# Where the next values are made: moving small steps of a fused attention and expert kernel around its last batch

## The chip, the cores and the metric

One core of one Trainium2 chip. The metric is the device time of one launch in microseconds, median of three runs.

## The reference

One model step on 16 sequences of 256 tokens, width 128, in float32: a long convolution, a mixture of experts, an attention, and the same mixture of experts again, each added to its input after a layer norm.

```python
x = x + conv(layernorm(x), ...)          # state-space convolution by FFT
x = x + ffn(layernorm(x), ...)           # 8 experts, hidden 256, top 2 of a softmax
x = x + attention(layernorm(x), ...)     # 16 heads of 8, 4 query sets, causal
x = x + ffn(layernorm(x), ...)           # the same experts

# ffn
w, idx = top_k(softmax(x @ Wg + bg), 2);  w = w / sum(w)
comb = sum(one_hot(idx) * w)
h = relu(einsum(x, W1) + b1);  y = einsum(h, W2) + b2
out = einsum(y, comb)
# attention: for each of 4 query sets, with shared keys and values
att = softmax(causal(q @ k.T * scale));  y = att @ v
out = concat(y) @ W_proj.T
```

## The kernel before

The 4096 tokens are 32 tiles of 128. All intermediate data stays in the core's memory. Each engine runs one long list of instructions, written out by hand in the order of its queue; semaphores with constant thresholds connect them. There is no planner. The phases are: filter taps and convolution, the first expert pass, the attention, and the second expert pass.

**Expert passes** (`tensor_first`, `tensor_second` and their like on the other engines). 8 chunks of 4 tiles, 8 experts each. For an expert PE runs `tensor_up` (L718, two halves of three matmuls, into PSUM banks 0 to 3), ScalarE `scalar_relu` (L732 and L734, four instructions), VectorE and GpSimd form low parts (L741, L748), and two experts later PE runs `tensor_down` (L766, 24 matmuls of 128 columns, into banks 4 and 5 in turn), which VectorE adds into `mixed`, weighted by `comb_y` (`vector_accumulate`, L778). `tensor_down` waits for the accumulation two experts before, and each accumulation for the one before it. Between the experts of a chunk stand the routing steps of the next: norm statistics (`vector_route_stats`, L324 and L328), a reciprocal root on GpSimd (`gpsimd_route_rstd`, L333 and L335), `vector_route_normed` (L341), transposition (`tensor_xt`, L591), `tensor_logits` (L616), `vector_top` (L623 to L634), an exponential of the gap (`scalar_gap`, L639), `vector_combine` (L645 to L667), `tensor_comb_t` (L676), its copy `scalar_comb_t` (L684), the biases weighted by the router (`tensor_base`, L691) and their addition to the stream (`vector_base`, L699). Chunk 0 of the second pass has no pass of its kind before it, so its routing steps stand in the last batch element of the attention.

**Attention** (`tensor_attention` and its like). 16 batch elements, 16 steps each, numbered n from 0 to 255. A step on PE: `tensor_scores(n)` (L1013, three matmuls of 512 columns) into banks 0 to 2 or 3 to 5 in turn, which waits until ScalarE is done with step n - 2; then what stands beside it (`tensor_beside`); then the weighing of the values of four steps earlier (`tensor_weigh`, L1064, into bank 7): none at n % 4 == 0, one, two and one at the following steps. ScalarE runs one `scalar_exp` (L1022, 128x1536) for each step, GpSimd masks its result (L1032 to L1040), VectorE turns the outputs of four steps (`vector_turn`, L1072 to L1077) at n % 4 == 3, and the next weighing waits for the turn. Scores 1 wait for the last accumulation of the first pass, since its output stands in bank 5.

**Beside the steps** of batch element b, by step number: the transposition of element b + 2 at 0 (`tensor_at_x`, L865, which waits until the values of b are copied out of bank 6), its queries and keys at 4, 8 and 12 (`tensor_qk`, L906, and on VectorE `vector_qk_high` L931 and `vector_qk_low` L936), the output projection of element b - 1 at 7 and 11 (`tensor_project`, L1119, `vector_attended`, L1129), and the values of element b + 1 at 14:

```python
        if b + 1 < BATCH and at == 14:
            tensor_v(e, b + 1)
```

`tensor_v` (L970, six matmuls into bank 6) waits for the last `vector_qk_low`, and `vector_v` (L989) copies its result. In the last element the projections stand at 10 and 11. Norm statistics and normalization of later chunks stand beside these steps too.

**Seam to the second pass.** `tensor_second` weighs the last four sums with `tensor_up(0, 0)` and `tensor_up(0, 1)` between them, and projects the last element after expert 2 of chunk 0.

Of the kernel before, what the change touches and what calls it, by code (L numbers as in the profile page):

```python
# [17 lines left out]
P = 128  # L18
# [98 lines left out]
def build_in(nc, dr, out, ctx):  # L117
# [523 lines left out]
    def vector_combine(e, m, ch):  # L641
# [13 lines left out]
        last.then_inc(routed, 1)  # L655
        e.wait_ge(routed, at + 9)
# [10 lines left out]
        e.tensor_scalar(comb_y[:, s], comb[:, s], 1.0 if m.whole else 1.0 / WSCALE, None, ALU.mult).then_inc(routed, 1)  # L667

# [81 lines left out]

    def tensor_down(e, m, ch, ex):
        i = (m.at + ch) * EXPERTS + ex
        r, to = i % HRING, bank(4 + i % 2)
# [8 lines left out]
        if i >= 2:  # L762
            e.wait_ge(accum, i - 1)
        for t in range(FFN_TILES):
# [5 lines left out]
    def vector_accumulate(e, m, ch, ex):  # L770
# [6 lines left out]
        for t in range(FFN_TILES):  # L777
            last = e.scalar_tensor_tensor(out=m.y[:, t0 + t, :], in0=bank(4 + i % 2)[:, t * P:(t + 1) * P],  # L778
# [217 lines left out]
    def tensor_scores(e, n):  # L996
        b, c, t = step_of(n)
        s, to = b % 2, psum[:, TILE * (n % 2):TILE * (n % 2 + 1)]
        if n >= 2:
            e.wait_ge(exped, n - 1)  # L1000
        elif n == 1:
            e.wait_ge(accum, EXPERTS * FFN_CHUNKS)
        else:
            e.wait_ge(relued, HBLK * EXPERTS * FFN_CHUNKS)
# [45 lines left out]
    def tensor_weigh(e, n):  # L1050
# [5 lines left out]
        if n == 0:  # L1056
            e.wait_ge(based, FFN_CHUNKS)
# [48 lines left out]
    def tensor_project(e, b, h):  # L1106
# [5 lines left out]
        elif b + 3 == BATCH:  # L1112
            e.wait_ge(attn_done, HALVES * b + 1)
        elif b + 2 == BATCH:
            e.wait_ge(combt_copied, FFN_CHUNKS + 1)
# [7 lines left out]
    def vector_attended(e, b, h):  # L1123
        tile = HALVES * b + h

        e.wait_ge(projected, tile + 1 if b + 2 < BATCH else HALVES * (b + 1))
# [239 lines left out]
    def tensor_second(e):  # L1366
# [8 lines left out]
        for ch in range(FFN_CHUNKS):  # L1375
            for ex in range(EXPERTS):
                if ch or ex >= 2:
                    tensor_up(e, second, ch, ex)
                if due := lagging(ch, ex):
# [16 lines left out]
    def scalar_second(e):  # L1396

        e.wait_ge(scored, LAST)
        for ch in range(FFN_CHUNKS):
            for ex in range(EXPERTS):  # L1400
                scalar_relu(e, second, ch, ex)
                if ch + 1 < FFN_CHUNKS:
                    scalar_route(e, second, ch + 1, routing_step(ch + 1, ex))

    def vector_second(e):
        for ch in range(FFN_CHUNKS):
            for ex in range(EXPERTS):
                vector_low(e, second, ch, ex)
                if (ch, ex) == (0, 0):
                    vector_turn(e, LAST // 4 - 1)  # L1410
                    vector_rows(e, BATCH - 1)
                if due := lagging(ch, ex):
# [10 lines left out]
                if (ch, ex) == (1, 4):  # L1423
                    vector_route_stats(e, second, FFN_CHUNKS - 1)
                if (ch, ex) == (1, 7):
                    vector_route_normed(e, second, FFN_CHUNKS - 1)
# [13 lines left out]
    def gpsimd_second(e):  # L1440
        for ch in range(FFN_CHUNKS):
            for ex in range(EXPERTS):
                gpsimd_low(e, second, ch, ex)
                if (ch, ex) == (1, 5):
                    gpsimd_route_rstd(e, second, FFN_CHUNKS - 1)
# [15 lines left out]
    def tensor_beside(e, b, at):  # L1461
# [6 lines left out]
        if b + 1 < BATCH and at == 14:  # L1468
            tensor_v(e, b + 1)
        if b + 1 == BATCH:  # L1470
# [5 lines left out]
            elif at == 8:  # L1476
                tensor_comb_t(e, second, 0)
            elif at in (10, 11):
                tensor_project(e, b - 1, at - 10)
            elif at == 14:  # L1480
# [372 lines left out]
```

## Time and profile before

| | |
|---|---|
| median of 3 runs | 875.84 us (875.54 to 876.68) |
| profiled execution | 874.92 us |
| its span, first to last instruction | 873.2 us |
| granted TensorE clock, mean over the span | 0.992 of 2.4 GHz |
| busy: PE / ScalarE / VectorE / GpSimd | 94% / 83% / 75% / 63% |
| first pass, attention, second pass start at about | 95, 291, 670 us |

PE is TensorE's matmuls, PEld its weight loads, DVE VectorE, ACT ScalarE, POOL GpSimd, SP SyncE. Times in the trace are microseconds from the start of the span. Matmuls are pipelined and their ends modelled, so a listed duration can run into the next instruction. An idle time in brackets is that of the engine before the instruction, with the instruction that ended it. Rows of busy time by stretch list the stretch, its length, the busy microseconds and number of instructions of PE, PEld, DVE, ACT and POOL, the granted TensorE clock as a share of 2.4 GHz, the DMA engines' share and GB/s.

### The profile page before, as it was taken

What the parts mean: (1) busy time and instruction counts of PE and PEld (TensorE: products, weight loads), DVE (VectorE), ACT (ScalarE), POOL (GpSimd) and SP (SyncE); (2) the same over time, 40 slices, a digit from 0 to 9 for tenths busy, and PEclk for the clock granted to TensorE, in tenths of its full rate; (3) what the DMA queues carried; (4) which work ended last, traced back from release to release, by engine and by line L of the source; (5) the groups of instructions that cost most, each with busy time, mean ns of one, the idle gap of its engine ahead of it and who ended that gap; (6) DMA issues with size and microseconds to landing.
All of it is one profiled execution on the core that took longest, in us unless ns stands there. A gap on an engine that the chain in (4) does not pass through costs nothing.

```text
span 873.2 us, 20943 instructions
## 1 busy us (share of the span) xinstructions
PE 825.0 (94%) x7953; PEld 465.6 (53%) x7953; DVE 657.1 (75%) x1966; ACT 727.7 (83%) x918; POOL 549.7 (63%) x620
## 2 busy tenths in 40 slices
PE   5899999999999899999999999999989999999995
PEld 4644577777777433333333333333223777777774
DVE  6898689988987566777777777777565888777775
ACT  7630588888898799999999999999997788988884
POOL 1177455555543688888888888888885454444432
PEclk9999999999999899999999999999999999999999
DMA  8101100000003334434444433355300000000000
GB/s 282 33 1 48 49 2 2 2 2 2 2 16 84 98 82 92 85 93 83 98 90 98 90 83 85 96 99 98 97 1 2 2 14 14 14 14 13 14 14 15
DMA packets 38408, 46.00 MB, mean 53 GB/s; under 512 B 6680, under 2 KB 24352, under 8 KB 38304
## 3 DMA queue, kind: packets, MB, share of 16 engines
q1 hardware_dynamic: 38304, 44.62, 21.5%
q8 instruction: 64, 1.05, 0.6%
q14 instruction: 40, 0.33, 0.1%
HBM read 27.83 MB, written 16.78 MB: 51 GB/s over the span
## 4 chain that ended last, share of the span: by engine, by line
PE 69%; DVE 13%; ACT 10%; issue 4%; POOL 2%; SPq 0%; DMA 0%; ACTq 0%
PE psum L766 18%; PE psum L718 17%; PE psum L1064 13%; ACT prob L1022 7%; PE psum L1013 5%; PE psum L1119 4%; DVE normed L341 3%; PE psum L545 2%; POOL prob L1037 2%; ACT decay L409 2%; PE psum L906 2%; DVE o_tok L1072 2%; PE psum L691 2%; PE psum L616 1%; PE psum L512 1%
## 5 line engine op out<-in xcount | busy, mean ns | idle before, releaser
L1022 ACT ACTIVATE prob<-psum 128x1536 f32<-128x1536 f32 x256 | 349.7, 1474 | 26.7 <-PE psum L1013 26.7
L1064 PE MATMUL psum<-prob,vstack 128*32 128x256 f32 (+1 forms) x2048 | 206.9, 499 | 2.6 <-DVE o_tok L1072 2.6
L718 PE MATMUL psum<-xt_parts,w_parts 128*128 128x512 f16 x768 | 186.8, 379 | 0.0
L778 DVE SCALAR_TENSOR_TENSOR mixed<-psum,comb_y,mixed 128x128 f32<-128x128 f32 x512 | 143.5, 342 | 2.1 <-PE psum L766 2.1
L748 POOL TENSOR_TENSOR hidden_parts_second<-hidden_second,hidden_parts_second 128x512 f16<-128x512 f32 x64 | 78.0, 1219 | 104.5 <-ACT hidden_parts_second L734 104.5
L748 POOL TENSOR_TENSOR hidden_parts_first<-hidden_first,hidden_parts_first 128x512 f16<-128x512 f32 x64 | 80.0, 1253 | 82.6 <-ACT hidden_parts_first L734 82.6
L732 ACT ACTIVATE hidden_first<-psum,b 128x512 f32<-128x512 f32 x128 | 88.2, 689 | 26.7 <-PE psum L718 19.1
L1032 POOL TENSOR_SCALAR_AFFINE_SELECT prob<-prob 128x512 f32<-128x512 f32 x128 | 82.4, 644 | 43.7 <-ACT prob L1022 38.3
L732 ACT ACTIVATE hidden_second<-psum,b 128x512 f32<-128x512 f32 x128 | 88.4, 691 | 25.2 <-PE psum L718 23.8
L1013 PEld LDWEIGHTS psum<-qstack,kstack 32*128 32x128 f16 x768 | 24.8, 91 | 157.0 <-ACT prob L1022 117.2
L1013 PE MATMUL psum<-qstack,kstack 32*128 32x512 f16 x768 | 100.9, 390 | 8.0 <-POOL prob L1037 3.6
L718 PEld LDWEIGHTS psum<-xt_parts,w_parts 128*128 128x128 f16 x768 | 71.3, 99 | 65.4 <-issue 2.2
L1072 DVE STREAM_TRANSPOSE o_tok<-psum 128x512 f32<-128x512 f32 x64 | 45.8, 716 | 71.5 <-PE psum L1064 71.4
L766 PEld LDWEIGHTS psum<-w_parts,hidden_parts_first 128*128 128x128 f16 x1536 | 90.9, 98 | 16.1 <-issue 1.9
L766 PEld LDWEIGHTS psum<-w_parts,hidden_parts_second 128*128 128x128 f16 x1536 | 91.0, 98 | 15.2 <-issue 0.6
L766 PE MATMUL psum<-w_parts,hidden_parts_first 128*128 128x128 f16 x1536 | 96.0, 219 | 0.7 <-DVE mixed L778 0.6
L766 PE MATMUL psum<-w_parts,hidden_parts_second 128*128 128x128 f16 x1536 | 96.0, 219 | 0.5 <-POOL hidden_parts_second L748 0.5
L1037 POOL TENSOR_SCALAR_AFFINE_SELECT prob<-prob 128x1280 f32<-128x1280 f32 x64 | 85.1, 1330 | 5.8 <-ACT prob L1022 1.2
L734 ACT ACTIVATE hidden_parts_second<-psum,b 128x512 f16<-128x512 f32 x128 | 88.5, 692 | 0.0
L734 ACT ACTIVATE hidden_parts_first<-psum,b 128x512 f16<-128x512 f32 x128 | 88.3, 690 | 0.0
L1034 POOL TENSOR_SCALAR_AFFINE_SELECT prob<-prob 128x512 f32<-128x512 f32 x128 | 82.5, 645 | 0.0
L741 DVE TENSOR_TENSOR hidden_parts_second<-hidden_second,hidden_parts_second 128x512 f16<-128x512 f32 x64 | 44.9, 702 | 42.2 <-ACT hidden_parts_second L734 42.1
(116 smaller groups left out, 1110.2 us busy)
## 6 DMA issues: line engine op xcount, KB each, us to landing
qstack<-qk_parts SPq DMA_DIRECT2D x128, 128.0 KB, 3.6
qk_parts<-parts SPq DMA_DIRECT2D x64, 192.0 KB, 3.2
kstack<-qk_parts SPq DMA_DIRECT2D x128, 32.0 KB, 3.6
stream<-L_attn_a_u SPq DMA_DIRECT2D x4, 512.0 KB, 7.5
kept_x<-stream SPq DMA_DIRECT2D x4, 512.0 KB, 2.6
out<-mixed SPq DMA_DIRECT2D x8, 256.0 KB, 2.3
w_whole<-L_ffn_W SPq DMA_DIRECT2D x1, 1024.0 KB, 7.4
taps<-c_taps SPq DMA_DIRECT2D x1, 640.0 KB, 8.4
```

The costliest lines, as they stand in the source:

```text
L718: last = e.matmul(bank(u % 4), m.w1[:, w_part, ex, cols], xt_parts[:, s, x_part, :], start=(n == 0), stop=(n == len(PRODUCTS) - 1))
L732: last = e.activation(m.hidden[:, r, k, :], bank(u % 4), ACT.Relu, scale=scale, bias=bias)
L734: last = e.activation(m.hidden_parts[:, r, 0, k, :], bank(u % 4), ACT.Relu, scale=scale, bias=bias)
L748: e.tensor_tensor(m.hidden_parts[:, r, 1, 1, :], m.hidden[:, r, 1, :], m.hidden_parts[:, r, 0, 1, :], ALU.subtract).then_inc(low_second, 1)
L766: last = e.matmul(to[:, t * P:(t + 1) * P], h_[:, t * P:(t + 1) * P], w_, start=(n == 0), stop=(n == len(terms) - 1))
L778: last = e.scalar_tensor_tensor(out=m.y[:, t0 + t, :], in0=bank(4 + i % 2)[:, t * P:(t + 1) * P], scalar=comb_y[:, s, t, ex:ex + 1], in1=m ...
L1013: last = e.matmul(to[:, i * BANK:(i + 1) * BANK], kstack[at, s, c, keys * P:(keys + 1) * P], queries, start=True, stop=True)
L1022: e.activation(prob[:, n % PROBS, :], psum[:, TILE * (n % 2):TILE * (n % 2 + 1)], ACT.Exp, scale=SCALE)\
L1032: e.affine_select(blocks[:, 0:3:2], blocks[:, 0:3:2], [[0, 2], [0, 2], [1, P]], ALU.is_ge, 0.0, base=0, channel_multiplier=-1)
L1034: e.affine_select(blocks[:, 4:6], blocks[:, 4:6], [[0, 2], [0, 2], [1, P]], ALU.is_ge, 0.0, base=0, channel_multiplier=-1).then_inc(masked, 1)
L1037: e.affine_select(blocks[:, 0:5], blocks[:, 0:5], [[0, 5], [0, 2], [1, P]], ALU.is_ge, 0.0, base=0, channel_multiplier=-1).then_inc(masked, 1)
L1064: last = e.matmul(to[SLOT * lane:SLOT * (lane + 1)], vstack[:, b % 2, keys, first:first + SLOT], weights_of(n - t, lane, keys, pair), star ...
```

## The change

Five edits to the order of the queues and one to a buffer:

- `tensor_v` of the next element stands beside step 15 instead of 14. VectorE's copy stays in its list at step 14, in front of the turn of step 15.
- The output of the last `tensor_down` of the first pass goes to bank 7 instead of 5 (`down_bank`). Scores 1 wait for one accumulation less, the first weighing for all.
- In the last element the projections stand at 8 and 11, and each attended tile waits for its own projection. `vector_combine` is cut in two, `vector_pick` at step 8 and `vector_comb` at step 12.
- `tensor_comb_t`, `scalar_comb_t`, `tensor_base` and `vector_base` of the second pass's chunk 0 move into the second pass, at its experts 0 and 1.
- The norm of chunk 6 moves from the last element into chunk 0 of the second pass (statistics at expert 4, root at 5, normalization at 7), as that of chunk 7 already stood in chunk 1.

```diff
+    def down_bank(m, i):
+        return 7 if m is first and i == EXPERTS * FFN_CHUNKS - 1 else 4 + i % 2
...
     def tensor_down(e, m, ch, ex):
         i = (m.at + ch) * EXPERTS + ex
-        r, to = i % HRING, bank(4 + i % 2)
+        r, to = i % HRING, bank(down_bank(m, i))
...
+        if down_bank(m, i) == 7:
+            e.wait_ge(based, FFN_CHUNKS)
...
     def tensor_scores(e, n):
         elif n == 1:
-            e.wait_ge(accum, EXPERTS * FFN_CHUNKS)
+            e.wait_ge(accum, EXPERTS * FFN_CHUNKS - 1)
...
     def tensor_weigh(e, n):
         if n == 0:
-            e.wait_ge(based, FFN_CHUNKS)
+            e.wait_ge(accum, EXPERTS * FFN_CHUNKS)
...
     def tensor_project(e, b, h):
+        elif b + 2 == BATCH and h == 0:
+            e.wait_ge(routed, STEPS * FFN_CHUNKS + 1)
         elif b + 2 == BATCH:
-            e.wait_ge(combt_copied, FFN_CHUNKS + 1)
+            e.wait_ge(attn_done, HALVES * b + 1)
...
     def vector_attended(e, b, h):
-        e.wait_ge(projected, tile + 1 if b + 2 < BATCH else HALVES * (b + 1))
+        e.wait_ge(projected, tile + 1 if b + 1 < BATCH else HALVES * (b + 1))
...
     def tensor_second(e):
+                if (ch, ex) == (0, 0):
+                    e.wait_ge(attn_done, HALVES * (BATCH - 1))
+                    tensor_comb_t(e, second, 0)
+                if (ch, ex) == (0, 1):
+                    tensor_base(e, second, 0)
...
     def scalar_second(e):
                 scalar_relu(e, second, ch, ex)
+                if (ch, ex) == (0, 0):
+                    scalar_comb_t(e, second, 0)
...
     def vector_second(e):
+                if (ch, ex) == (0, 1):
+                    vector_base(e, second, 0)
...
-                if (ch, ex) == (1, 4):
-                    vector_route_stats(e, second, FFN_CHUNKS - 1)
-                if (ch, ex) == (1, 7):
-                    vector_route_normed(e, second, FFN_CHUNKS - 1)
+                if ch < 2 and ex == 4:
+                    vector_route_stats(e, second, FFN_CHUNKS - 2 + ch)
+                if ch < 2 and ex == 7:
+                    vector_route_normed(e, second, FFN_CHUNKS - 2 + ch)
...
     def gpsimd_second(e):
-                if (ch, ex) == (1, 5):
-                    gpsimd_route_rstd(e, second, FFN_CHUNKS - 1)
+                if ch < 2 and ex == 5:
+                    gpsimd_route_rstd(e, second, FFN_CHUNKS - 2 + ch)
...
     def tensor_beside(e, b, at):
-        if b + 1 < BATCH and at == 14:
+        if b + 1 < BATCH and at == 15:
             tensor_v(e, b + 1)
...
-            elif at == 8:
-                tensor_comb_t(e, second, 0)
-            elif at in (10, 11):
-                tensor_project(e, b - 1, at - 10)
-            elif at == 14:
-                e.wait_ge(attn_done, HALVES * (BATCH - 1))
-                tensor_base(e, second, 0)
+            elif at in (8, 11):
+                tensor_project(e, b - 1, at // 10)
...
     def scalar_attention(e):
-            elif n == LAST - STEPS_B + 8:
-                scalar_comb_t(e, second, 0)
...
     def vector_beside(e, b, at):
-        if 0 < b < BATCH - 1 and at in (6, 10):
-            vector_attended(e, b - 1, at // 8)
-        if b + 1 == BATCH and at in (9, 10):
-            vector_attended(e, b - 1, at - 9)
+        if b and at in (6 if b + 1 < BATCH else 9, 10):
+            vector_attended(e, b - 1, at // 10)
...
-        if b % 2 and b >= 3:
+        if b % 2 and 3 <= b < BATCH - 1:
...
-            elif at == 6:
-                vector_combine(e, second, 0)
-            elif at == 14:
-                vector_base(e, second, 0)
+            elif at == 8:
+                vector_pick(e, second, 0)
+            elif at == 12:
+                vector_comb(e, second, 0)
```

## Rows read from the trace of the kernel before

**Rows 1.** Busy time by stretch: batch 1, last batch, a second-pass chunk.

```profile
338.23:361.37 23.14, 22.33 (x219) 8.17 (x215) 16.91 (x38) 21.81 (x16) 20.03 (x27) 1.00 0.45 92
640.53:670.07 29.54, 24.88 (x228) 8.97 (x227) 19.87 (x57) 23.95 (x21) 22.24 (x29) 0.94 0.01 2
694.30:718.30 24.00, 24.00 (x254) 17.84 (x252) 20.76 (x78) 19.81 (x36) 13.15 (x11) 1.00 0.05 13
```

**Rows 2.** Timeline of ScalarE: start, duration, operation, idle time before.

```profile
315.10 12.20 ACT L1022 ACTIVATE prob<-psum 128x1536 f32<-128x1536 f32 x9 [0.50 <-PE psum L1013]
...
356.85 4.13 ACT L1022 ACTIVATE prob<-psum 128x1536 f32<-128x1536 f32 x3 [0.66 <-PE psum L1013]
361.37 12.20 ACT L1022 ACTIVATE prob<-psum 128x1536 f32<-128x1536 f32 x9 [0.39 <-PE psum L1013]
...
593.86 12.20 ACT L1022 ACTIVATE prob<-psum 128x1536 f32<-128x1536 f32 x9 [1.04 <-PE psum L1013]
```

**Rows 3.** Timeline around step 14 of batch 1, PE and VectorE.

```profile
358.68 0.69 DVE L936 SCALAR_TENSOR_TENSOR parts<-psum,parts 128x512 f16<-128x512 f32 x1
...
359.43 0.51 PE L970 MATMUL psum<-wqkv_parts,at_x 128*128 128x128 f16 x6 [0.61 <-DVE parts L936]
...
359.87 1.07 PE L1064 MATMUL psum<-prob,vstack 128*32 128x256 f32 x16
...
360.87 0.39 PE L1013 MATMUL psum<-qstack,kstack 32*128 32x512 f16 x3
...
361.19 1.07 PE L1064 MATMUL psum<-prob,vstack 128*32 128x512 f32 x8
```

**Rows 4.** Timeline at the seam from the first pass to the attention.

```profile
294.05 0.61 PE L1013 MATMUL psum<-qstack,kstack 32*128 32x512 f16 x6 [1.00 <-DVE mixed L778]
...
299.81 1.94 PE L1064 MATMUL psum<-prob,vstack 128*32 128x512 f32 x8
...
302.34 12.26 ACT L1022 ACTIVATE prob<-psum 128x1536 f32<-128x1536 f32 x9 [0.96 <-PE psum L1013]
```

**Rows 5.** Busy time by stretch: attention's start, small operations of the last batch.

```profile
295.00:300.00 5.00, 3.27 (x19) 1.23 (x23) 1.56 (x8) 5.00 (x5) 3.79 (x6) 0.55 0.44 101
649.94:652.04 2.10, 2.10 (x29) 0.70 (x27) 2.00 (x7) 1.74 (x2) 2.10 (x4) 0.87 0.00 0
```

**Rows 6.** Timeline of the last batch, from step 6 on.

```profile
649.94 0.84 DVE L645 CAST top_no<-top_at 128x8 f32<-128x8 uint32 x1
...
650.24 4.30 ACT L1022 ACTIVATE prob<-psum 128x1536 f32<-128x1536 f32 x3 [0.41 <-PE psum L1013]
...
654.52 0.60 PE L676 MATMUL psum<-eye,comb 128*8 128x128 f32 x4 [1.56 <-DVE comb L665]
...
657.27 1.16 PE L1119 MATMUL psum<-wproj,o_rows 128*128 128x128 f32 x8
...
659.86 1.45 ACT L1022 ACTIVATE prob<-psum 128x1536 f32<-128x1536 f32 x1 [0.96 <-PE psum L1013]
...
668.64 1.50 PE L1064 MATMUL psum<-prob,vstack 128*32 128x512 f32 x16 [0.84 <-DVE o_tok L1072]
```

**Rows 7.** Timeline: comb_t's copy, the last projections, the biases of chunk 1.

```profile
655.16 0.57 ACT L684 COPY comb_t<-psum 8x512 f32<-8x512 f32 x1 [0.62 <-PE psum L676]
...
677.47 2.05 PE L1119 MATMUL psum<-wproj,o_rows 128*128 128x128 f32 x16 [0.23 <-DVE o_rows L1087]
...
694.37 1.15 PE L691 MATMUL psum<-b,comb_t 8*128 8x128 f32 x8
```

**Rows 8.** Timeline of the second pass: accumulation and statistics.

```profile
690.99 1.11 DVE L778 SCALAR_TENSOR_TENSOR mixed<-psum,comb_y,mixed 128x128 f32<-128x128 f32 x4
...
692.93 1.50 PE L766 MATMUL psum<-w_parts,hidden_parts_second 128*128 128x128 f16 x24
...
712.20 0.86 DVE L324 BATCH_NORM_STATS2 stats<-stream 128x6 f32<-128x128 f32 x4
713.10 0.38 DVE L328 BATCH_NORM_AGGREGATE meanvar<-stats 128x2 f32<-128x6 f32 x4
```

More of the change, by code:

```diff
@@ L639, in scalar_gap, with vector_pick @@
         e.activation(gap[:, s, :], gap[:, s, :], ACT.Exp).then_inc(gap_exp, 1)
-    def vector_combine(e, m, ch):
+    def vector_pick(e, m, ch):
         n, s = m.at + ch, ch % 2
@@ L655, in vector_combine, with vector_comb @@
         last.then_inc(routed, 1)
+    def vector_comb(e, m, ch):
+        n, s = m.at + ch, ch % 2
+        at = STEPS * n
         e.wait_ge(routed, at + 9)
@@ L667, in vector_combine @@
         e.tensor_scalar(comb_y[:, s], comb[:, s], 1.0 if m.whole else 1.0 / WSCALE, None, ALU.mult).then_inc(routed, 1)
+    def vector_combine(e, m, ch):
+        vector_pick(e, m, ch)
+        vector_comb(e, m, ch)
     def tensor_comb_t(e, m, ch):
@@ L777, in vector_accumulate @@
         for t in range(FFN_TILES):
-            last = e.scalar_tensor_tensor(out=m.y[:, t0 + t, :], in0=bank(4 + i % 2)[:, t * P:(t + 1) * P],
+            last = e.scalar_tensor_tensor(out=m.y[:, t0 + t, :], in0=bank(down_bank(m, i))[:, t * P:(t + 1) * P],
                                           scalar=comb_y[:, s, t, ex:ex + 1], in1=m.y[:, t0 + t, :], op0=ALU.mult,
@@ L1557, in gpsimd_attention @@
                 gpsimd_mixed_rstd(e, b // 2 + 2)
-            if at == 3 and b % 2 and b >= 3:
+            if at == 3 and b % 2 and 3 <= b < BATCH - 1:
                 gpsimd_route_rstd(e, second, (b - 3) // 2)
```

## The prediction

> **What bounds the kernel now.** I read the page first, then the busy time by stretch, then ScalarE's timeline through the attention, and only then all engines around the places that the diff touches.
>
> The attention is 256 steps, 16 to a batch element (a "batch" below). A step is one `scalar_exp` of 1.45 us on ScalarE. A batch lasts 23.14 us, of which ScalarE is busy 21.81 and PE 22.33 [rows 1]: both are nearly full, so the question is which is late at each step. ScalarE's rows answer it: the exps come in unbroken runs, and each run begins with an idle time that ended with L1013, the scores on PE [rows 2]. Three exps in a row last 4.13, so one follows the next after (4.13 - 1.45) / 2 = 1.34 us; they overlap by 0.11, and a pause costs its listed idle time plus 0.11. So ScalarE sets the end, and PE adds a pause wherever it had too much work between two scores. A PE step is 0.32 for the scores (360.87 to 361.19) and 1.00 for the weighing (359.87 to 360.87) [rows 3]; every fourth step has no weighing. An exp starts 0.50 after its scores (360.87 to 361.37). A listed PE duration runs some 0.07 into the next instruction (1.07 against 1.00), which I take off below.
>
> One pause of each batch stands where the change works. At step 14 PE stands 0.61 us until L936 has made the low parts, then runs the six matmuls of the next values (L970, 0.44 to the next instruction), then the weighing, and only then the scores of step 15 [rows 3]. Exp 15 starts at 361.37, with 0.39 idle before it [rows 2].
>
> The last batch is another case: 29.54 us up to the second pass's first matmul, at a mean clock of 0.94. A chunk of the second pass has PE busy through all of its 24.00 us, with VectorE at 20.76 [rows 1]. What is added to PE there counts in full; what is added elsewhere counts where PE comes to wait.
>
> **Part 1, values in step 15.** I count from the start of exp 12 (356.85). Without its stand, PE would begin the product at 359.43 - 0.61 - 0.07 = 358.75. With the product gone from there, the weighing begins then and scores 15 come 1.00 later, at 2.9. Exp 15 could start at 3.4; its turn on ScalarE is 3 x 1.34 = 4.03, and in the rows it starts at 4.52. So the pause goes if step 15 can carry the product: 2.9 + 0.32 + 0.44 + 1.00 puts scores 16 at 4.7, exp 16 could start at 5.2 and is due at 5.37. It fits, with 0.18 to spare. The low parts are ready at 2.5 (358.68 + 0.69) [rows 3], before the product's new place at 3.2, so the stand goes too. In step 16 the next transposition needs the copied values: the copy (a VectorE instruction of some 0.4, an estimate from 128x512 in 0.69) ends at about 4.2, the transposition comes at 5.0. VectorE now stands for the copy in front of the turn. The turn waits for the weighing of step 15, which ends at 4.7, so the copy is done by then, and nothing else is queued between.
>
> The saving is one pause in each of the batches 0 to 13; 14 and 15 have no product that waits for L936. The first costs 0.50 + 0.11. In batch 12 VectorE is late with L936 through the weight ranges, and the pause costs 1.04 + 0.11; L936 is ready there some 0.65 later than elsewhere, at 3.2, just in time for the new place. The twelve others cost 0.39 + 0.11 [rows 2]. 0.61 + 1.15 + 12 x 0.50 = **-7.8 us**. Bounds: nothing, if the pause only moves; 7.8, if none is left.
>
> **Part 2, last outputs in bank 7.** Scores 1 stand 1.00 us for the last accumulation of pass one, because its bank is one of theirs [rows 4]. With that output in bank 7 they wait for the one before, which is done: 1.00 earlier. The weighing that now waits for bank 7 comes at 299.81, long after. But the gain meets a slow clock: TensorE's granted clock is 0.55 on average from 295 to 300 [rows 5], so 1.2 GHz for most of it. The weighing takes 1.94 instead of 1.07, and exp 6 starts at 302.34 after 0.96 idle [rows 4]. If the slow stretch stays in its place, one more microsecond of PE work falls into it, and by exp 7 some 0.4 of the 1.0 is left. I take **-0.6** (0.4 to 1.0).
>
> **Part 3, the last batch.** Removed from it: comb_t at step 8 with PE's wait of 1.56 for VectorE, its copy on ScalarE, the biases, VectorE's share of them, and the norms of chunk 6. The two projections (1.16, so 1.09) move from steps 10 and 11 to 8 and 11. I walk it from exp 6 at 650.24 [rows 6]. Three exps take 4.30 there, so exp 8 starts at 653.09 and its scores at 652.6. Step 8 is now 0.32 + 1.09: scores 9 at 654.0, exp 9 at 654.5, 0.07 late. Steps 9 and 10 are 1.32 each: exp 10 at 655.8, exp 11 at 657.2. Step 11 is 0.32 + 1.09 + 1.00: scores 12 at 659.05, exp 12 at 659.55, a pause of 1.04, such as a projection makes today (0.96 idle at 659.86). PE goes on: step 12 (no weighing) to 659.4, the wait for the turn to 660.1, steps 13 to 15 to 663.8, and the wait for the turn in front of the last matmuls as now (0.84 idle in its row, 0.9 with the overlap): 664.7 in place of 668.64, **-3.9 us**. It needs VectorE to be done with the picks and the first attended tile when the projection comes at 657.0. The turn of step 7 should end there at about 654.2; VectorE's work from 649.94 to 652.04, mostly these small operations, is 2.1 us [rows 5], so they end at 656.3 and the tile at 656.6. Bounds: -2.9, if they take a microsecond more; -4.9, if the clock stays full in this batch.
>
> The page "SBUF — State Buffer" of the Trainium skill (section "Who interferes with whom") has a rule against this step: a VectorE instruction with two SBUF inputs, or a cast in a two-port mode, and a GpSimd one that reads SBUF shut each other out, each for the whole of the other. The cast at 649.94 takes 0.84 for 8 elements a partition, with GpSimd busy throughout, which agrees. By the rule alone each of three picks could stand behind a whole mask, and the projection would be a microsecond late: the sum would be 1 us higher. By the row it is not.
>
> **Part 4, comb_t and biases in the second pass.** They now stand on PE between the attention's last weighing and `tensor_up(0, 2)`. From comb_t's start to the start of its copy are 0.64 (654.52 to 655.16), the copy takes 0.57, and PE goes on some 0.2 later: 1.4. Nothing of PE's queue can pass this wait. The biases take 1.15, 1.08 net [rows 7]. Of these 2.5 us, what PE stands today before the last projections is hidden: 0.23 in the row of 677.47, about 0.4 with the overlap. **+2.1 us** (1.7 to 2.6). ScalarE stands too, because the copy is queued between relu 0 and relu 1; but relu 1 is next wanted by `tensor_up(0, 3)`, two ups, a down and two projections later. VectorE's addition of the biases is in time for chunk 1's transposition, for the same reason.
>
> **Part 5, norms in the second pass.** Statistics and aggregation cost VectorE 0.86 + 0.38 = 1.24 at expert 4, behind `vector_combine` in the same expert. Today the accumulation of expert 3 ends at 690.99 + 1.11 = 692.1, and `tensor_down` of expert 5, which waits for it, starts at 692.93 [rows 8]: 0.83 to spare. 1.24 - 0.83 = 0.4, with contention **+0.5** (0 to 1.2). The normalization at expert 7 precedes nothing that PE wants soon, and GpSimd, with 13.15 busy of 24.00 [rows 1], has room for its two operations.
>
> **The sum** is -7.8 - 0.6 - 3.9 + 2.1 + 0.5 = -9.7 us. The profiled execution took 874.92 (span 873.2 and 1.7 around it), 0.9 under the median of 875.84 and 0.6 under the fastest of the three. -9.7 gives 865.2 for a profiled run and **866.1 us** for the median.
>
> **Rivals.** (a) *The pause moves instead of closing.* If the product takes 0.7 in step 15 instead of 0.44, or the transposition of step 16 stands for the copy, exp 16 is late by what exp 15 gained, in each batch, and the 7.8 is lost: 873.9. For it: the margin of 0.18. Against: scores, product and weighing have their measured lengths, and the copy has 0.8 to spare.
>
> (b) *More is lost at the seam.* The picks are late, or TensorE's clock falls to 1.2 GHz in the thin work of part 4 (a stand, small matmuls). At the other seam it was at 1.2 GHz soon after PE stood 1.00 [rows 4, 5], and a weighing took 0.87 longer; in a part that PE bounds this costs 1 to 1.7. With one or both, +2.3: 868.4.
>
> The skill's page "TensorE: Matmul & The Clock Gate" (section "Why this matters for your kernels") ties a fall to a long idle gap between bursts of matmuls. The stand at 294.05 was short, so the trace doesn't agree that only long ones matter. By the page the clock part of this rival costs nothing; by the row it can.
>
> (c) *Slower: the clock falls in every batch.* PE's stand and its work change places in step 14 and 15. If that takes the clock to 1.2 GHz once a batch, each fall costs a pause as in rows 4, 0.96 + 0.11 = 1.07; fourteen are +15.0, and the sum is +5.3: 881.1. It decides from ten falls on. Against: the clock is 1.00 in a whole batch [rows 1] in spite of a stand of 0.61, which now goes away.
>
> **Chances.** The forecast 0.74 (own range 863.8 to 869, by the bounds above without all of them at once), (b) 0.15, (a) 0.08, in part or in full, (c) 0.03. The range 863.5 to 870.3 leaves out (c), most of (a) and some of the low end. Within 0.2% (1.8 us) this kernel can't be told from no change; (a) in full stands at that limit. Faster 0.93, same 0.04, slower 0.03.
>
> **What would show it.** A batch takes 22.6 us in place of 23.14, with two pauses (exps 8 and 12) instead of three, and L970 has no idle time before it. Scores 1 start at 293.0. From the first exp of the last batch to `tensor_up(0, 0)` it is 25.6 instead of 29.5. Then PE stands some 0.9 us before L691, and the second pass takes 2.6 more than today. The forecast is wrong if a pause appears before exp 16, if the last batch has pauses beside the one at its exp 12, or if the clock is under 1 in the second pass.

## The result and the profile after

The changed kernel takes **863.0 us** (median of 6 runs, 861.68 to 864.4), the kernel before 876.37 beside it (6 runs, 875.54 to 876.96): a ratio of 0.9848, interval 0.9836 to 0.9861, or 13.4 us less. Forecast were 866.1 and a range from 863.5; the direction was right, the gain 3.7 too small and outside the range.

The profiled execution took 863.78 us (span 862.0, mean granted clock 0.992), 11.1 less than that of before. So two profiles differ by 2.3 us less than the medians do, and that gap is most of what has to be explained. Three executions among all the runs below, two of the kernel before (1048.9 and 1361.55 us) and one of the changed kernel with added matmuls (2047.37 us), were slow and are left out of the ratios.

Busy time by stretch: batch 1 (counted, as in [rows 1], from its exp 15 to the next batch's exp 15), the attention's start, and the last batch from its first exp to `tensor_up(0, 0)`. They answer to [rows 1, 5]. Counted from exp 0, the step in [rows 3] is one of batch 2 and not of batch 1; the batches are alike there.

```profile
335.04:357.68 22.64, 22.34 (x219) 8.18 (x215) 17.10 (x39) 21.70 (x18) 19.95 (x27) 1.00 0.48 94
295.00:300.00 5.00, 4.05 (x23) 1.24 (x23) 1.99 (x8) 4.99 (x4) 4.80 (x7) 0.66 0.40 116
630.81:656.24 25.43, 23.33 (x217) 7.75 (x215) 13.55 (x44) 23.06 (x20) 21.07 (x27) 0.93 0.00 1
```

ScalarE's timeline, from exp 1 and in the last batch [rows 2, 4, 6]:

```profile
293.10 6.89 ACT L1036 ACTIVATE prob<-psum 128x1536 f32<-128x1536 f32 x5 [0.74 <-PE psum L1027]
300.27 24.32 ACT L1036 ACTIVATE prob<-psum 128x1536 f32<-128x1536 f32 x18 [0.28 <-PE psum L1027]
324.87 5.48 ACT L1036 ACTIVATE prob<-psum 128x1536 f32<-128x1536 f32 x4 [0.28 <-PE psum L1027]
331.01 16.23 ACT L1036 ACTIVATE prob<-psum 128x1536 f32<-128x1536 f32 x12 [0.66 <-PE psum L1027]
347.52 5.48 ACT L1036 ACTIVATE prob<-psum 128x1536 f32<-128x1536 f32 x4 [0.28 <-PE psum L1027]
...
640.48 8.33 ACT L1036 ACTIVATE prob<-psum 128x1536 f32<-128x1536 f32 x6 [0.41 <-PE psum L1027]
649.73 5.48 ACT L1036 ACTIVATE prob<-psum 128x1536 f32<-128x1536 f32 x4 [0.92 <-PE psum L1027]
```

Where [rows 2] have runs of 3 and 9 exps with 0.39 between, there is now one of 12 (331.01): the pause before exp 15 is gone, and none came before exp 16. Exp 6 starts after 0.28 idle instead of 0.96. In the last batch the 0.41 before exp 6 is as it was, and the only other pause is one of 0.92 before its exp 12.

PE's timeline, the last batch's weighing and projections, then the seam and the accumulation behind the norm's statistics [rows 6 to 8]:

```profile
637.90 1.94 PE L1078 MATMUL psum<-prob,vstack 128*32 128x512 f32 x8
...
643.09 1.16 PE L1136 MATMUL psum<-wproj,o_rows 128*128 128x128 f32 x8
...
647.14 1.16 PE L1136 MATMUL psum<-wproj,o_rows 128*128 128x128 f32 x8
...
654.80 1.50 PE L1078 MATMUL psum<-prob,vstack 128*32 128x512 f32 x16 [0.84 <-DVE o_tok L1086]
...
660.60 0.60 PE L684 MATMUL psum<-eye,comb 128*8 128x128 f32 x4
...
661.87 1.15 PE L699 MATMUL psum<-b,comb_t 8*128 8x128 f32 x8 [0.66 <-ACT comb_t L692]
...
681.49 1.50 PE L780 MATMUL psum<-w_parts,hidden_parts_second 128*128 128x128 f16 x24 [0.32 <-DVE mixed L792]
```

PE stands nowhere for the router in the attention any more, and one weighing took 1.94 instead of 1.07: in this execution the clock was at 1.2 GHz there. VectorE's small operations of the router at step 8, behind the turn, with `comb` of step 12, and what GpSimd did beside the first of them:

```profile
642.90 0.72 DVE L1086 STREAM_TRANSPOSE o_tok<-psum 128x512 f32<-128x512 f32 x1 [2.03 <-PE psum L1078]
...
644.53 0.16 DVE L645 CAST top_no<-top_at 128x8 f32<-128x8 uint32 x1
...
645.38 0.72 DVE L653 TENSOR_TENSOR pick<-expert_no,top_no 128x32 f32<-128x32 f32 x2
646.02 0.28 DVE L1146 TENSOR_TENSOR stream<-psum,mixed 128x128 f32<-128x128 f32 x1
...
651.17 0.19 DVE L669 TENSOR_TENSOR comb<-pick 128x32 f32<-128x32 f32 x1
```

```profile
643.46 0.87 POOL L1054 TENSOR_SCALAR_AFFINE_SELECT prob<-prob 128x768 f32<-128x768 f32 x1
644.80 0.64 POOL L1046 TENSOR_SCALAR_AFFINE_SELECT prob<-prob 128x512 f32<-128x512 f32 x1 [0.47 <-ACT prob L1036]
```

Cut at the same events (exps 0, 6, 15 and 240, the second pass's first up, first down and sixth down), the difference of the two profiles is: part 1 (exps 15 of batches 0 to 13) -7.7, part 2 (exp 0 to exp 6) -1.7, last batch -4.1, comb_t and biases in the second pass +1.9, norm +0.5, sum -11.1. The last two can't be parted in this pair: from the first up to the first down it is 2.35 longer, from there to the sixth down 0.05. They are parted by the run further down that moves comb_t and the biases and not the norm: +2.35 and -0.44 there, so +0.49 is left for the norm.

### The profile page after: what moved, and what is told of

Its sections match the earlier page's. It is cut to its first block, busy times and chain, and to the rows that moved or that the text cites. A ratio compares the mean times of both kernels' runs of the same rounds, so it can differ in the third digit from the quotient of the medians.

```text
span 862.0 us, 20945 instructions
## 1 busy us (share of the span) xinstructions
PE 824.6 (96%) x7953; PEld 465.9 (54%) x7953; DVE 655.3 (76%) x1966; ACT 726.0 (84%) x918; POOL 550.8 (64%) x620
## 4 chain that ended last, share of the span: by engine, by line
PE 66%; ACT 14%; DVE 9%; issue 7%; POOL 3%; SPq 0%; DMA 0%; ACTq 0%
PE psum L780 17%; PE psum L726 16%; PE psum L1078 12%; ACT prob L1036 11%; PE psum L1027 5%; PE psum L1136 4%; DVE normed L341 3%; PE psum L545 2%; POOL prob L1051 2%; PE psum L920 2%; PE psum L699 2%; PE psum L616 1%; DVE mixed L792 1%; PE psum L512 1%; DVE prod L524 1%
```

## The experiments

**Each part alone.** Three kernels, each with one group of the edits, and one with all but part 2.

```diff
e1_values (part 1)
-        if b + 1 < BATCH and at == 14:
+        if b + 1 < BATCH and at == 15:
             tensor_v(e, b + 1)
e2_bank7 (part 2)
-        r, to = i % HRING, bank(4 + i % 2)
+        r, to = i % HRING, bank(down_bank(m, i))
...
-            e.wait_ge(accum, EXPERTS * FFN_CHUNKS)
+            e.wait_ge(accum, EXPERTS * FFN_CHUNKS - 1)
e3_seam (parts 3 to 5): projections at 8 and 11, pick at 8, comb at 12,
        comb_t, biases and the norm of chunk 6 in the second pass
e4_no_bank7: the changed kernel without the edits of e2_bank7
```

> The kernel before with tensor_v in step 15 alone (part 1). Sum of the pauses: 7.8 us less, so a ratio of 0.991, in the median as in the profile, with L970 without idle time and no pause before exps 15 and 16. If the 3.7 us that the changed kernel gained beyond the forecast come from part 1, more than 9 us less. If they come from the seams and TensorE's clock there, exactly 7.8, and the same slow stretches as before (near 295 and near 647 less the shift).

> The kernel before with the last outputs of pass one in bank 7 alone (part 2). By the forecast 0.6 us less (0.4 to 1.0). By the theory that PE's stand of 1.00 at the seam is what lets the clock fall for so long, 1.7 or more: scores 1 come 1.00 earlier, the slow stretch is half as long, and exp 6 has 0.3 idle before it instead of 0.96. A median that gains more than the profile would say that the slow stretch is missing in some executions.

> The kernel before with the edits of the last batch and the second pass (parts 3, 4 and 5) and nothing else. By the forecast -3.9 + 2.1 + 0.5 = 1.3 us less; by the profile of the changed kernel -4.1 + 1.9 + 0.5 = 1.7 less. If the surplus of the median lies in the clock of this seam, 2.5 to 4 less in the median.

> The changed kernel without bank 7: parts 1, 3, 4 and 5. If the parts add up, e1 and e3 together: 9.1 us less than before by the forecast, 9.5 by the profile. Against the changed kernel it shows bank 7 once more: 0.6 slower by the forecast, 1.7 to 3.5 slower by the clock theory.

| | median us (runs) | ratio to before, interval |
|---|---|---|
| part 1 alone | 867.72 (6) | 0.99, 0.9887 to 0.9914 |
| part 2 alone | 874.86 (11) | 0.9984, 0.9975 to 0.9993 |
| parts 3 to 5 alone | 872.47 (5) | 0.9959, 0.9945 to 0.9973 |
| all but part 2 | 864.97 (4) | 0.9874, 0.9859 to 0.9889 |

Against 876.53 beside them these are -8.8, -1.7, -4.1 and -11.6. The parts add up to -14.6 against the -13.4 of all, and part 1 and parts 3 to 5 to -12.9 against the -11.6 of the kernel with both; most of what is too much lies in part 1, for which the interval (-9.9 to -7.5) holds the forecast as well. Part 2 is worth -1.7 alone (interval -2.2 to -0.6) and -2.0 (863.0 - 864.97) on top of the rest, where -0.6 was forecast. Parts 3 to 5 are -4.1 together, where the sum had -3.9 + 2.1 + 0.5 = -1.3: here lies the largest miss. The profile of part 1 alone had a last batch of 32.44, though nothing in it was edited; that of parts 3 to 5 one of 24.13.

**Matmuls to hold the clock.** If the miss is the clock, matmuls put where PE stands should hold it. They are added to both kernels: four of 512 columns beside each of steps 2 and 3, and in the last batch at step 2, in the kernel before also at step 0. Their results are not used.

```diff
+            if n == 0:
+                e.wait_ge(based, FFN_CHUNKS)
+                tensor_fill(e, 7)
+            if n in (2, 3):
+                e.wait_ge(accum, EXPERTS * FFN_CHUNKS)
+                tensor_fill(e, 7)
+            if n == LAST - STEPS_B + 2:
+                e.wait_ge(xt_high, FFN_CHUNKS + 1)
+                tensor_fill(e, 6)
```

> The kernel before with extra matmuls, whose results nobody reads, where PE stands at the two seams: four of 512 columns into bank 7 at steps 0, 2 and 3 of the attention, and four into bank 6 at step 2 of the last batch. They cost 0.86 us each time at full clock, where ScalarE sets the pace. By the clock theory the slow stretches at the seams get rarer and the kernel gets faster by 1 to 3 us with a mean clock above 0.994. If TensorE's clock has no share in it, no change, or up to 2 us slower.

> The changed kernel with the same extra matmuls, except at step 0, where bank 7 is in use. By the clock theory it gains less than the kernel before does by them, 0 to 1.5 us, because it has fewer slow stretches, and the distance between the two filled kernels is 10 to 11.5 us, what the queues alone give, in place of 13.4. If the distance stays at 13.4, the surplus is none of the clock.

Before with them: 875.49 (12 runs; ratio 0.9995, 0.9986 to 1.0005), which can't be told from no change, where 1 to 3 us less were expected. Changed with them: 862.35 (6 runs; 0.9844, 0.9828 to 0.986). The distance stayed at 13.1; it did not shrink to the expected 10 to 11.5. By the words of the expectation that speaks against the clock, but the profiles show that the matmuls missed the place where it falls. In both the clock is 1.00 from the first exp on through 15 steps (21.89 us for them in the kernel before, against 23.86 and 23.17 in two profiles without), but the old last batch still took 31.09 at a mean clock of 0.95. These matmuls held the clock at the first seam and, in the new order, in the last batch (24.13, clock 1.00), not in the old order, where it falls later, behind step 8. So something in that order, behind step 8, goes with the fall there; what it is, the next runs show.

**Comb_t behind the first up; the values' product twice.** Two checks on single terms, in the changed kernel.

```diff
e7_combt_early, tensor_second:
         tensor_up(e, second, 0, 0)
+        e.wait_ge(attn_done, HALVES * (BATCH - 1))
+        tensor_comb_t(e, second, 0)
         tensor_weigh(e, LAST - 2)
...
e9_twice, tensor_v:
-        for h in range(HALVES):
+        for h in (0, 1, 0, 1):
```

> The changed kernel with tensor_comb_t behind tensor_up(0, 0), so that ScalarE copies it right after relu 0 and the biases find it ready. The stand of PE before the biases (0.66) and of ScalarE before the copy (1.68) should go: 1.2 us less (part 4 then costs 1.1 instead of 2.35). If part 4's price is PE's own work alone, no gain.

> The changed kernel with the value product made twice over, 12 matmuls instead of 6 (0.44 us more in step 15). By the walk of step 15 it has 0.18 us to spare: exp 16 comes 0.26 late in each of 14 batches, 3.6 us, and the product of the first pass costs 0.4 once: 4 us slower in all. If the step had no room, 14 x 0.44 = 6.2 slower; if PE had room beyond the walk, less than 1.

Comb_t early: 862.81 (0.9846, 0.9828 to 0.9865). From the first up to the first down are 7.19 in place of 8.02: 0.8 is there in the profile, where 1.2 were expected; the medians differ by 0.2, less than they can tell. Product twice: 865.1 (0.9876, 0.9858 to 0.9894), +2.1 and not +4. From exp 16 to exp 240, 14 batches, the profile is 1.62 longer, 0.12 each, for 0.44 more work. Step 15 has 0.44 - 0.12 = 0.32 to spare, not 0.18.

**Comb_t moved alone.** Every profile of the old order shows PE standing at step 8 for VectorE's router result. In the kernel before, only comb_t, its copy and the biases go to the second pass; two more runs are the kernel before and the changed kernel again.

```diff
     tensor_beside, last batch
-            elif at == 8:
-                tensor_comb_t(e, second, 0)
...
     tensor_second
+                if (ch, ex) == (0, 0):
+                    e.wait_ge(attn_done, HALVES * (BATCH - 1))
+                    tensor_comb_t(e, second, 0)
...
```

> The kernel before with one thing alone: comb_t, its copy and the biases of the second pass's chunk 0 stand in the second pass; the router's combination stays whole at step 6, the projections at 10 and 11, the norm of chunk 6 in the attention. Theory (the last batch fell to 1.2 GHz in one or two stretches because PE stood some 2 us for comb_t there): with that stand gone the last batch takes 25 to 25.5 us from its first exp to the second pass's first up, with no slow stretch behind its step 9, part 4 gives 2 back, and the median is 3.5 to 4 under the kernel before. Rival (only the order of the work counts, as in the forecast's sum): 1.5 to 2 under it, with a slow stretch still in the last batch.

> The kernel before once more, for another look at its last batch. Theory (the profiled execution was a lucky one): 31 to 32.5 us from the batch's first exp to the second pass's first up. Rival (29.5 is what this kernel does, and the three other looks at the old order owe their 31 to 32.4 to their own edits): 29.5 again.

> The changed kernel once more, for another look at its last batch: 24.1 with no stretch at 1.2 GHz or 25.4 with one, never above 26, if the old order alone had the longer ones.

The theory fell: **878.98** (12 runs; 1.0023, 1.0011 to 1.0035), slower than before by 2.6, where 3.5 to 4 less was expected. Its profile is 2.3 longer than that of the kernel before again (878.7 against 876.4). The last batch is 0.9 of a microsecond shorter (30.18 against 31.07), the second pass pays the 1.9 of part 4, and 1.2 more lie behind the last down of the kernel, where nothing was edited. PE's timeline in that run:

```profile
652.36 0.39 PE L1013 MATMUL psum<-qstack,kstack 32*128 32x512 f16 x3 [0.37 <-ACT prob L1022]
655.75 1.53 PE L1064 MATMUL psum<-prob,vstack 128*32 128x512 f32 x8 [2.99 <-DVE o_tok L1072]
657.21 0.61 PE L1013 MATMUL psum<-qstack,kstack 32*128 32x512 f16 x3
657.75 2.04 PE L1119 MATMUL psum<-wproj,o_rows 128*128 128x128 f32 x8
```

and VectorE's:

```profile
648.41 1.24 DVE L1087 STREAM_TRANSPOSE o_rows<-o_norm 128x1024 f32<-128x1024 f32 x1
...
649.74 0.84 DVE L645 CAST top_no<-top_at 128x8 f32<-128x8 uint32 x1
...
651.84 1.15 DVE L658 TENSOR_TENSOR pick<-pick,wpair 128x32 f32<-128x32 f32 x2
653.02 1.25 DVE L665 TENSOR_TENSOR comb<-pick 128x32 f32<-128x32 f32 x1
654.30 0.78 DVE L667 TENSOR_SCALAR comb_y<-comb 128x32 f32<-128x32 f32 x1
654.99 0.70 DVE L1072 STREAM_TRANSPOSE o_tok<-psum 128x512 f32<-128x512 f32 x1
```

PE no longer waits for comb, so it waits 2.99 us for the turn instead, which is queued on VectorE behind the whole of `vector_combine`: ten instructions, from 649.74 to 655.08. Several of them last until a mask of GpSimd beside them ends. These are the masks beside `comb` and `comb_y`:

```profile
652.90 1.32 POOL L1037 TENSOR_SCALAR_AFFINE_SELECT prob<-prob 128x1280 f32<-128x1280 f32 x1
654.18 0.86 POOL L1040 TENSOR_SCALAR_AFFINE_SELECT prob<-prob 128x768 f32<-128x768 f32 x1
```

The addition that starts at 653.02 ends 0.05 behind the first mask, at 654.27; in the changed kernel, where no mask runs at its start (651.17), it takes 0.19. The stand was not comb_t's alone; it is VectorE's queue at steps 6 and 7. Behind the stand the projection takes 2.04 instead of 1.16. The kernel before, profiled again, shows the same with comb_t in front:

```profile
654.28 0.60 PE L676 MATMUL psum<-eye,comb 128*8 128x128 f32 x4 [2.32 <-DVE comb L665]
...
655.71 1.57 PE L1064 MATMUL psum<-prob,vstack 128*32 128x512 f32 x8 [0.51 <-DVE o_tok L1072]
...
657.76 2.00 PE L1119 MATMUL psum<-wproj,o_rows 128*128 128x128 f32 x8
```

Its last batch took 31.07 (31 to 32.5 was expected, 29.5 by the rival), that of the changed kernel again 25.42.

**Which edit removes the stand.** From both sides: the cut of the combination added to the last kernel, taken out of the changed one, and taken out while the order behind the turn is kept.

```diff
e11_cut (on e10_combt_moved), and e12_whole the reverse (on the changed kernel)
-            elif at == 6:
-                vector_combine(e, second, 0)
+            elif at == 8:
+                vector_pick(e, second, 0)
+            elif at == 12:
+                vector_comb(e, second, 0)
e13_whole_at_8 (on the changed kernel)
             elif at == 8:
-                vector_pick(e, second, 0)
-            elif at == 12:
-                vector_comb(e, second, 0)
+                vector_combine(e, second, 0)
```

> The kernel before with comb_t and the biases in the second pass (as in the run just before) and, beyond that, one edit: the router's combination is cut in two, its picks at step 8 and the rest at step 12 of the last batch, behind the turns. Projections stay at 10 and 11, the norm of chunk 6 in the attention. Theory (VectorE's uncut combination at step 6 held the turn of step 7, and PE stood for whichever of the two it wanted first): PE's stand of 2.99 at step 8 goes, the last batch takes 25 to 27 us in place of 30.2, with no slow stretch of the clock behind step 9, and the median is 4 under the run with comb_t moved, 873 to 875.5. Rival (the projections' places or the norm made the last batch long): it stays at 29 or more, and the median at 877 or more.

> The changed kernel with one edit undone: the combination whole at step 6, in front of the turn of step 7. Theory: the turn ends some 3 us late, PE stands for it at step 8, and the clock falls behind the stand; the last batch takes 28 to 30 us in place of 24.1 to 25.4, the median is 3.5 to 5.5 above the changed kernel, 866.5 to 868.5. Rival (the projections' new places did it): within 0.7 of the changed kernel, 863 to 863.7.

> The changed kernel with the combination whole, but at step 8, behind the turn of step 7: only the cut is undone, not the order. If the order behind the turn is what counts, the last batch takes 24 to 26 us and the median is 0 to 1.3 above the changed kernel, 863 to 864.3. If the cut counts (three more operations of up to 1.25 beside the masks, in front of the attended tile for which the second projection waits), PE stands at step 11 and it is 2 or more above, 865 or more.

| | median us (runs) | ratio to before, interval | last batch us | PE's longest stand for VectorE in it |
|---|---|---|---|---|
| comb_t moved | 878.98 (12) | 1.0023, 1.0011 to 1.0035 | 30.18 | 2.99, turn |
| + cut | 874.9 (11) | 0.998, 0.9971 to 0.9988 | 26.83 | 1.42, turn |
| changed, whole at 6 | 868.32 (6) | 0.9898, 0.9881 to 0.9916 | 28.50 | 2.83, turn |
| changed, whole at 8 | 867.45 (4) | 0.9888, 0.9873 to 0.9902 | 28.24 | 2.65, attended tile |
| changed | 863.0 (6) | 0.9848, 0.9836 to 0.9861 | 25.43 | 0.84, turn |

The cut alone gives back 4.1 by the medians, its undoing costs 5.3, and keeping only the order costs 4.4 (by the ratios 3.8, 4.4 and 3.5). Each is as the theory or, for the last, the second of its two branches had it, and in each pair the two intervals don't meet. The last batch alone shows it too: 3.35 shorter with the cut, 3.9 and 3.7 longer without it than the mean of 24.6 in the changed order (below). The last batches of the first four, by stretch, in the order of the table:

```profile
640.36:670.54 30.18, 23.61 (x216) 8.46 (x214) 19.43 (x56) 23.01 (x20) 22.39 (x29) 0.94 0.00 1
```

```profile
640.10:666.93 26.83, 22.04 (x217) 7.66 (x214) 19.75 (x56) 22.98 (x20) 22.38 (x29) 1.00 0.01 1
```

```profile
633.03:661.53 28.50, 23.54 (x216) 7.82 (x214) 15.47 (x44) 23.01 (x20) 20.97 (x27) 0.94 0.00 1
```

```profile
632.86:661.10 28.24, 23.54 (x217) 7.92 (x214) 16.07 (x44) 22.80 (x20) 21.13 (x27) 0.94 0.00 1
```

PE in the kernel with the combination whole at 6, then at 8:

```profile
648.32 1.25 PE L1078 MATMUL psum<-prob,vstack 128*32 128x512 f32 x8 [2.83 <-DVE o_tok L1086]
...
650.04 1.94 PE L1078 MATMUL psum<-prob,vstack 128*32 128x256 f32 x16
```

```profile
650.62 1.45 PE L1136 MATMUL psum<-wproj,o_rows 128*128 128x128 f32 x8 [2.65 <-DVE stream L1146]
652.00 1.94 PE L1078 MATMUL psum<-prob,vstack 128*32 128x512 f32 x8
```

Whole at 6, it stands in front of the turn; whole at 8, in front of the first attended tile, for which the second projection waits. Only in two pieces, at steps 8 and 12 with both attended tiles between them, does PE wait for neither. At 8 the ten instructions lie beside masks again, such as this cast, which ends 0.02 behind the mask beside it:

```profile
645.26 1.05 POOL L1054 TENSOR_SCALAR_AFFINE_SELECT prob<-prob 128x768 f32<-128x768 f32 x1
...
645.50 0.83 DVE L645 CAST top_no<-top_at 128x8 f32<-128x8 uint32 x1
```

The way from the old order to the new runs in three steps through the last batch: 31.07, with comb_t moved 30.18, with the cut 26.83, and with the projections at 8 and 11 and the norm gone as well (the run of parts 3 to 5) 24.13. The cut is the largest step, not the whole; the last one, 2.7, was not parted further.

In each case a stand of over 2 us is followed by matmuls at 1.2 GHz and a mean clock of 0.94; without one it is 1.00 (+ cut).

**A better version?** From the changed kernel, comb_t behind the first up and the norm's statistics one expert later; and in a second kernel comb_t in the stand of 0.84 before the last weighings.

```diff
e8_both (on e7_combt_early)
-                if ch < 2 and ex == 4:
+                if (ch, ex) in ((0, 5), (1, 4)):
                     vector_route_stats(e, second, FFN_CHUNKS - 2 + ch)
...
e14_stand (on e8_both), tensor_second
+        e.wait_ge(attn_done, HALVES * (BATCH - 1))
+        tensor_comb_t(e, second, 0)
         tensor_weigh(e, LAST - 4)
...
```

> The changed kernel with comb_t behind the first up of the second pass and the statistics of chunk 6's norm one expert later, its root too. By the single terms: 0.8 for comb_t (its profile showed that) and 0.4 for the statistics, so 1.2 under the changed kernel, 861.8; 0 to 0.4 if the accumulations behind the statistics are late at expert 5 as they were at expert 4.

> The best version so far (comb_t behind the first up, the norm's statistics one expert later) with comb_t moved on into the place in front of the last two weighings of step 255, where PE stands 0.84 us for the turn, and its copy in front of the first relu. Its matmuls (0.53) are then hidden and the copy's wait too: 0.5 under that version, 861.7. Rival: nothing is gained if the copy makes the first relu late or the turn's wait grows.

862.27 (5 runs; 0.9838, 0.9825 to 0.9851) and 862.35 (5 runs; 0.9832, 0.9817 to 0.9846), where 861.8 and 861.7 were expected. In the profiles the terms are there: first up to first down 8.02, 7.19 and 6.76, and 0.49 for the statistics. The medians are 0.7 below the changed kernel's and can't be told from it: between the executions of one kernel, taken over all kernels, the time rises by some 0.4 us for each 0.001 that the mean granted clock is lower, and the same kernel's executions lie between 0.991 and 0.997.

## Why the prediction was wrong, by its steps

| step | forecast | measured |
|---|---|---|
| part 1, values in step 15 | -7.8 | -7.7 by the profiles, -8.8 by the medians |
| part 2, bank 7 | -0.6 | -1.2 by the mean of the profiles, -1.7 and -2.0 by the medians |
| part 3, last batch | -3.9 | -6.5 by the mean of the profiles |
| part 4, comb_t and biases | +2.1 | +1.9 |
| part 5, norm | +0.5 | +0.5 |
| sum | -9.7 | -13.0 by the profiles; medians -13.4 |

**The step that failed is part 3's term.** Its walk forward was right: 25.6 to `tensor_up(0, 0)`, measured 25.43 in the first profile of the changed kernel; projections at steps 8 and 11 on time; a pause of 1.04 at exp 12, measured 0.92 idle and 0.11; 0.84 before the last weighings. That it agrees so closely is in part luck, since this profile has the slow stretch around step 5 that the walk took over from [rows 6], and six of nine don't. What was wrong is the length from which it was taken, -3.9 where the profiles have -6.5. The 29.5 of [rows 1] belong to one execution. Five profiles of the old last batch gave 29.51, 31.07 (before again), 32.44 (part 1 alone), 31.37 (part 2 alone) and 31.09 (with fillers): mean 31.1.

Nine at the new order gave 25.43, 25.42 and 25.49 (comb_t early), and six from 24.09 to 24.13 (one of them with fillers): mean 24.6. The difference is -6.5; of the 2.6 beyond the forecast 1.6 are the old order's (31.1 against 29.5), 1.0 the new one's (24.6 against 25.6). These are few profiles, one of each run, so the means are good to some tenths at best. The profiled pair happened to be the old order's shortest and one of the new order's longest.

Why the shortest: in the old order PE meets VectorE's queue at step 8, whatever it did before. In all five profiles comb_t starts 13.95 to 13.96 us behind the batch's first exp, with a slow stretch before it or without. In [rows 6] the matmuls at 1.2 GHz lay in front of that meeting (a weighing of 1.94 at step 5), where they only shortened the stand, from 2.32 to 1.56. In the other profiles the clock fell behind the stand, and from comb_t to the first up it took 17.1 to 18.5 us instead of 15.6. The prediction read the stand of 1.56 as comb_t's, on PE's queue. It is that of `vector_combine` before the turn; comb_t moved alone left a stand of 2.99 and took only 0.9 from the last batch. The walk held because it had the turn end at 654.2 with the combination gone from before it, though it named comb_t as what was removed.

The bound "-4.9, if the clock stays full" saw the clock only in the new order (the six profiles at a full clock are 5.4 under 29.5); nothing in the sum let the old one be longer than its one profile. The same holds for "0.9 under the median": that execution's distance to the median was carried over as if the changed kernel kept it. Beside the second profile of the same kernel it was 1.5 shorter, with 1.6 of it in the last batch, which the change rebuilds, and 0.7 lost at the attention's start.

**Part 2** was mis-sized as well: "if the slow stretch stays in its place" took 0.4 of the 1.0 away. In the changed kernel's profile the rows after the seam have a clock of 0.66 from 295 to 300 against 0.55, a weighing of 1.48 against 1.94 and 0.28 idle before exp 6. But there too the profile of before was one of several: it reached exp 6 11.10 us after exp 0, the same kernel again 10.44, the changed kernel 9.37. From exp 0 to exp 14, which no pause of part 1 touches, six profiles with bank 7 took 20.1 to 20.2 and three 21.4 to 21.8 (mean 20.6), and seven with bank 5 21.1 to 22.6 (mean 21.8), those with fillers left out: 1.2 less, the whole stand of 1.0 and a little.

**Parts 1, 4 and 5** stand as worked out. No pause came before exp 16 (rival a): the values' product found 0.32 spare. The clock didn't fall in the batches (rival c): 1.00 in the batch shown. Rival (b), a clock that falls in the thin work of part 4, didn't come about: from the first up to the first down it is 8.02 to 8.03 in each profile of that order.

The prediction weighed, and set aside "by the row", that VectorE and GpSimd shut each other out. The second projection was indeed on time, but the runs bear the exclusion out. In the last batch of all 18 profiles, 75 of the router's small operations took 0.5 us or more, up to 1.3, and each ended 0.02 to 0.05 behind an instruction of GpSimd. The cast took 0.16 in the three profiles in which GpSimd stood at its start, as in the 0.47 shown above, and 0.60 to 0.84 in the fifteen in which a mask ran. This agrees with the rule of the page "SBUF — State Buffer" of the Trainium skill (section "Who interferes with whom"). It didn't change the sum, because the picks at step 8 had time to spare: in the six profiles with a cast of 0.83 PE doesn't stand before the second projection either. Where PE waits behind these operations it costs: the ten instructions add up to 5.5 us in the kernel before, and whole at 8 to 4.9, against 2.8 or 3.3 in the changed order.

## What to carry to other kernels

When an engine stands for a result, look at what else is queued in front of what it will want next: taking away the wait named in the row can leave the stand as it is, under another name. A long group of small instructions in front of another engine's critical step can be cut in two, as here, and the pieces put where that step has been passed; how long they take also depends on what GpSimd runs beside them. And before a term is taken from one profiled stretch with a clock under 1.00, ask on which side of the next stand the slow part lay, since here it was free in front of it (comb_t at 13.96 either way) and cost 1.6 us and more behind it.

## What the runs showed of the hardware

TensorE's clock fell to 1.2 GHz at the seams in some executions and not in others: in the last batch of the new order, where the nine kernels differ little, three profiles have a mean of 0.93 and cost 1.3 us, six have 1.00. After a stand of 2.32 to 2.99 us it fell in each of the seven profiles that had one. The page "TensorE: Matmul & The Clock Gate" of the Trainium skill (section "Why this matters for your kernels") ties a fall to a long idle gap between bursts. In kind these runs agree for the stands of over 2 us; but at step 5 of the last batch it fell, where it did, behind one of 0.93 at step 3, which profiles without a fall have too. What decides there stays open, and no run parts a stand of over 2 us from what else is around it in these batches.

A small VectorE operation of the router that met a mask of GpSimd could take as long as the rest of the mask: one addition of 128x32 took 1.25 us beside one and 0.19 otherwise.
